# Cross-attention and expert mixture on one core: four gathers of 512 KB begun by two queues, queries made earlier, x loaded ahead of the gathers

## The reference

```
qk  = einsum('bhdq,bhdl->bhql', qh, kh) / sqrt(128)
ret = einsum('bhql,bhdl->bhdq', softmax(qk), vh)
x   = x + gamma * ret
```

```
h     = relu(xn @ W1 + b1);  alpha = softmax(h @ W2 + b2)
out   = sum_k alpha_k * U_k (V_k xn);   x = x + out
```

## Time and profile before

| | |
|---|---|
| median of 3 runs | 1813.11 us (1811.18 to 1814.56) |
| profiled execution | 1809.29 us, its span 1807.5 us |
| busy PE / VectorE / ScalarE / GpSimd | 1610.1 / 986.1 / 772.3 / 717.3 us |
| granted TensorE clock, mean | 0.967 |
| DMA moved by the sync queue | 293.87 MB |
| gather DMAs | 1024 of 128 KB, 2.8 us to landing |

### The profile page before, as it was taken

One profiled execution on the slowest core, in us unless ns is written; L12 is line 12 of the kernel. 1 busy time (PEld: TensorE's weight loads), 2 busy tenths in 40 slices (PEclk: granted clock), 3 DMA queues, 4 the chain that ended last, 5 costly groups with the idle time before them and its releaser, 6 DMA issues.

```text
span 1807.5 us, 22223 instructions
## 1 busy us (share of the span) xinstructions
PE 1610.1 (89%) x6496; PEld 1181.8 (65%) x6496; DVE 986.1 (55%) x1290; ACT 772.3 (43%) x1222; POOL 717.3 (40%) x523
## 2 busy tenths in 40 slices
PE   5888888887878888888887599999999999999999
PEld 3555555565656565656554478777787878787877
DVE  6767676768676777777776353242333333233312
ACT  5656565656656565656565341212212121212120
POOL 3767776777767777767675200000000000000000
PEclk9999999999999999999999799999999999999999
DMA  5877878778877878888877612112120303121202
GB/s 177 232 240 239 243 239 239 231 243 244 246 237 237 246 239 242 245 247 239 251 221 232 234 69 93 47 62 79 37 102 6 133 0 104 35 93 46 93 1 70
DMA packets 128155, 294.22 MB, mean 163 GB/s; under 512 B 34432, under 2 KB 39552, under 8 KB 128128
## 3 DMA queue, kind: packets, MB, share of 16 engines
q1 hardware_dynamic: 128128, 293.87, 53.2%
HBM read 125.87 MB, written 33.69 MB: 88 GB/s over the span
## 4 chain that ended last, share of the span: by engine, by line
PE 48%; SPq 16%; DVE 12%; DMA 9%; issue 8%; POOL 4%; ACT 1%; DVEq 0%; ACTq 0%; POOLq 0%
PE scores L929 19%; SPq L223 14%; PE scores L972 10%; PE attended L990 10%; DMA x_raw<-in_x 8%; DVE neg_max L571 6%; DVE pb L580 4%; POOL pt_lo L342 3%; PE scores L517 2%; PE spare L1009 2%; PE attended L539 1%; PE attended L542 1%; PE scores L944 1%; PE scores L947 1%; SPq L234 1%
## 5 line engine op out<-in xcount | busy, mean ns | idle before, releaser
L342 POOL TENSOR_TENSOR pt_lo<-pt,pt_hi 128x512 fp32r<-128x512 f32 (+1 forms) x256 | 399.9, 1563 | 247.2 <-ACT pt_hi L411 246.3
L418 ACT ACTIVATE probs<-scores,neg_max 128x1024 f32<-128x1024 f32 x256 | 285.8, 1117 | 322.6 <-DVE neg_max L571 322.5
L571 DVE TENSOR_REDUCE neg_max<-scores 128x1 f32<-128x1024 f32 x256 | 310.9, 1214 | 64.5 <-PE scores L517 63.8
L517 PE MATMUL scores<-k_hi,q_hi 128*128 128x512 f32 x512 | 235.8, 542 | 121.0 <-ACT probs L418 111.8
L580 DVE STREAM_TRANSPOSE pb<-probs 128x1024 f32<-128x1024 f32 x256 | 315.5, 1232 | 0.1
L854 POOL TENSOR_TENSOR rstd<-var_eps,minus_half 128x1 f32<-128x1 f32 x28 | 17.2, 615 | 609.4 <-DVE var_eps L1055 609.4
L517 PEld LDWEIGHTS scores<-k_hi,q_hi 128*128 128x128 f32 x512 | 97.7, 198 | 234.7 <-ACT probs L418 142.4
L411 ACT ACTIVATE pt_hi<-pt 128x512 fp32r<-128x512 f32 (+1 forms) x256 | 186.5, 728 | 56.4 <-DMA pt<-pb 56.4
L539 PE MATMUL attended<-pt_hi,v_hi 128*128 128x512 f32 x320 | 144.8, 453 | 70.0 <-POOL pt_lo L342 69.3
L542 PE MATMUL attended<-pt,v_nat 128*128 128x512 f32 x384 | 205.4, 617 | 0.0
L929 PE MATMUL scores<-nt_hi,w_hi 128*128 128x512 f32 x512 | 200.9, 392 | 2.5 <-DVE w_lo L1080 2.5
(11 more groups left out here) (95 smaller groups left out, 2709.2 us busy)
## 6 DMA issues: line engine op xcount, KB each, us to landing
pt<-pb SPq DMA_DIRECT2D x1024, 128.0 KB, 2.8
x_raw<-in_x SPq DMA_DIRECT2D x32, 512.0 KB, 5.6
k_raw<-in_ctx SPq DMA_DIRECT2D x32, 512.0 KB, 4.5
gain_row<-gains SPq DMA_DIRECT2D x64, 256.0 KB, 4.7
x_res<-in_x SPq DMA_DIRECT2D x32, 512.0 KB, 4.7
x<-x_out SPq DMA_DIRECT2D x64, 256.0 KB, 3.8
first_n<-x SPq DMA_DIRECT2D x32, 512.0 KB, 3.7
result<-x SPq DMA_DIRECT2D x64, 256.0 KB, 3.9
```

Source lines behind the costliest of these rows:

```text
L342: nc.gpsimd.tensor_tensor(pt_lo[2 * parity + half][:, :, keys, :], pt[2 * parity + half][:, :, keys, :], as_f32(hi[half][q][:]), ALU.subtr ...
L418: nc.scalar.activation(probs[j % 2][:], scores[j % 2][:], ACT.Exp, bias=neg_max[:, j:j + 1], accum_out=row_sum[b][:, j:j + 1]).then_inc(s_ ...
L517: last = mm(scores[j % 2][:, c * BANK:(c + 1) * BANK], q[b][:, queries], k[b][:, c * BANK:(c + 1) * BANK], start=(i == 0), stop=(i == 2))
L571: nc.vector.tensor_reduce(neg_max[:, j:j + 1], scores[j % 2][:], AX_X, ALU.max, negate=True).then_inc(s_max, 1)
```

## The change

The gather of a half becomes four DMAs of 512 KB, one for each source quadrant. The sync queue begins quadrants 0 and 1 where it began all 16 before. ScalarE begins quadrants 2 and 3: those of the last head's half 1 in block 1, after its `pt_hi`, and those of this head's half 0 in block 5. The semaphore's count for a gather goes from 256 to 64. On the sync queue the load of x for head h + 2 is moved ahead of the gather of half 0. ScalarE's `queries` and `high_queries` move from block 5 to block 3; VectorE's `variance` from block 3 to block 2, ahead of the scaling of attended; `scale_of_queries` from block 4 to 2 and `low_queries` from block 6 to 5 on GpSimd.

```diff
-    GATHERS = QB * QB * 16
+    GATHERS = QB * 16
@@ sync queue, gather
-            for g in range(QB):
-                for a in (0, 2, 1, 3):
-                    sp.dma_start(dst[g:P:QB, a, :, :].rearrange("p k n -> p (k n)"),
-                                 pb[half][SB * a:SB * a + SB, JB * g:JB * g + JB, :, :].rearrange(
-                                     "p k j c -> p (k j c)")).then_inc(s_gather[half], 16)
+            for a in range(QB // 2):
+                sp.dma_start(dst[:, a, :, :].rearrange("p k n -> p (k n)"),
+                             pb[half][SB * a:SB * a + SB, :, :, :].rearrange("p (g k) j c -> p g (k j c)", g=QB)
+                             ).then_inc(s_gather[half], 16)
@@ sync queue, slot
+            if more:
+                sp.wait_ge(s_q32, h + 2)
+                load_x(h + 2)
             gather(h, n, 0, parity)
             if not first:
                 spread_gain(h - 1, 1)
-            if more:
-                sp.wait_ge(s_q32, h + 2)
-                load_x(h + 2)
@@ GpSimd, slot
-                if j == 4 and not last:
+                if j == 2 and not last:
                     scale_of_queries(h + 1, 1 - parity)
-                if j == 6 and not last:
+                if j == 5 and not last:
                     low_queries(h + 1, 1 - parity)
@@ ScalarE
+        def gather(h, n, half, parity):
+
+            act.wait_ge(s_blocks, n + 4 * half + 4)
+            dst = pt[2 * parity + half]
+            for a in range(QB // 2, QB):
+                act.dma_start(dst[:, a, :, :].rearrange("p k n -> p (k n)"),
+                              pb[half][SB * a:SB * a + SB, :, :, :].rearrange("p (g k) j c -> p g (k j c)", g=QB)
+                              ).then_inc(s_gather[half], 16)
@@ ScalarE, slot
-                if j == 5 and not last:
+                if j == 1 and not first:
+                    gather(h - 1, n - JB, 1, 1 - parity)
+                if j == 5:
+                    gather(h, n, 0, parity)
+                if j == 3 and not last:
                     queries(h + 1, 1 - parity)
                     high_queries(h + 1, n + JB, 1 - parity)
@@ ScalarE, after the slots
+        gather(h - 1, n - JB, 1, 1)
         gains(h - 1, 0)
@@ VectorE, slot
-                if j == 3 and not last:
+                if j == 2 and not last:
                     dve.wait_ge(s_stat, h * 2 + 4)
...
+                if j == 2 and not last:
+                    variance(h + 1, 1 - parity)
                 if j == 2 and not early:
                     scale_attended(h - 2, n - 2 * JB, 1)
-                if j == 3:
-                    if not last:
-                        variance(h + 1, 1 - parity)
-                    if not first:
-                        inverse_sums(h - 1, 1, 1 - parity)
+                if j == 3 and not first:
+                    inverse_sums(h - 1, 1, 1 - parity)
```

## The result

The changed kernel takes 1826.72 us (median of 4 runs, 1823.01 to 1828.85) against 1812.14 before: a ratio of 1.0077 with a 95% interval of 1.0056 to 1.0098. It is slower by 0.8%, where 1634 us and a range of 1598 to 1690 were forecast. The profiled execution has a span of 1827.0 us. PE's granted clock over the run is 0.959, before it was 0.967.

What follows compares the result with a forecast made beforehand. No engine was taken as full: a loop through the sync queue's issue time and one late x load was the bound. 30 periods x 5.3 = 159 us plus 20 at the edges gave 179 us less: 1634 us, range 1598 to 1690.

Steps and rivals of the forecast that it cites:

- What bounds the kernel now: Attention stage: no engine full, but a loop through the sync queue's issue time and one late x load; period 30.51 us.
- The x load: Sync queue: x issued ahead of the gather, ending VectorE's stall of 6.2 us a head, 191.2 us in all.
- cover of 4.2 us: Time left for other traffic between x landing at 517.8 and VectorE first asking for it at 521.99.
- The gather on the sync queue: 16 issues become two of 0.6 us, so the queue is held 1.2 us instead of 10.2, twice a head.
- The gather on ScalarE: Blocks 1 and 5: four issues a head of 0.6 us, mostly fitting where ScalarE waited for the maxima.
- Rivals B and C: B: ScalarE's issues about 1.5 us each, 1712 us, chance 0.08; C: ScalarE held at every issue, 1880 us, chance 0.04.
- What is late next: PE's 23.4 us plus waits give 25.2 us a head; its block 5 pt_lo wait grows from 0.84 to about 1.5.
- Do the gathers land in time?: Next block 0: about 8.8 us available, 3 MB take 7.9 us at 397 GB/s; about 1.3 us lateness absorbed.
- Rival A: Gathers late: both halves together at 205 GB/s, so splitting quarter 0 ends the loop; 84 us more, 1718 us, chance 0.14.
- The port rule: Partitions 0 to 63 reach half of 16 DMA ports: sync queue's pair about 218 GB/s, full rate needing ScalarE's beside it.
- Edges: First and last slots: x wait 5 us less, VectorE's first_n wait 8 less, PE's last pt_lo wait 7 less.

Runs made afterwards that it cites:

- x ahead alone: Kernel after without its gather part: x load ahead and the reordering kept, 16 gathers of 128 KB a half on the sync queue; 1734.06 us, ratio 0.956.
- plain copies: Kernel after with every gather replaced by a same-size copy from each partition to the same partition (wrong values); 1647.36 us, ratio 0.9088.
- mixed pairs: Kernel after, but the sync queue takes quadrants 0 and 2 and ScalarE 1 and 3; 1792.24 and 1808.85 us.

## Why the prediction was wrong, point by point

- **What bounds the kernel now**: right. x ahead alone gives 0.956.
- **The x load**: the wait of 191.2 us was to vanish; after it is 72.5, or 2.5 us in each of 29. The cover of 4.2 us was eaten from two sides. The sync queue's store and residual issues, held for 2.46 and 2.11 us, let x go out at 524.32, 5.5 us before VectorE was ready for it (531.84 - 2.00), where 10.4 were forecast; and it took 7.5 us to land, not 6.2. With plain copies x lands in a median of 7.2 us and the wait is gone, so the late issue weighs more than the landing.
- **The gather on the sync queue**: "size hardly counts, and the sync queue is held 1.2 us". Wrong in the kernel after: single gather issues took a median of 1.0 and up to 4.7 us, the x load's a median of 2.6, and a gain's up to 4.0. Right with plain copies, 1.26 and 1.12 us for two.
- **The gather on ScalarE**: 0.6 us an issue was right (median 0.62 of 128, longest 3.6), and so was that it costs nothing: 25.61 us a head with plain copies. Rivals B and C are out.
- **What is late next**: 25.2 us a head against 25.61 measured where the DMA engines are not the limit, and PE's wait in block 5 1.19 us for the 1.5 forecast.
- **Do the gathers land in time?** This is the step that failed: "at the 397 GB/s reached where a gather ran beside a load that is 7.9 us ... I take the fast end." The 397 were one microsecond of a gather and the residual load together, and the row doesn't say how much was the gather. The row of the gather alone said 201 GB/s at a DMA share of 0.72; I read "not full". Divided, it is 201 / 0.72 = 280 GB/s for the old form (two queues made 270 of it alone, at a share of 0.87), and nothing at all was known of the new one. Measured alone, the new form makes 236 GB/s as the kernel begins it, and 167 to 236 over all orders. The transfer time of a whole head was never summed: with these rates it is 26.2 us, with the slowest full order 30.8, in both cases above PE's 23.4 and the forecast's 25.2. In place of 25.2 the runs show 31.27 us with the gathers and 25.61 with plain copies of the same size, so the missed term, what the gather's transfers cost beyond plain copies, is 5.7 us a head. The sum by the kernel's own form gives 0.6 of it (26.2 less 25.61); where the other 5.1 come from is open.
- **Rival A** named the mechanism with too small a price, and its sign came: ScalarE's wait for the gather of 5.90 us at 504.41. It took 205 GB/s for the two halves and let only one wait grow; in the kernel residual, x, `pb` and pt are late together. Its own row, 2 MB in 10.2 us, twice a head and 3.0 MB besides at 357 GB/s, adds up to 29 us. I never made that sum, though it would have been too high for the old form: the kernel with x ahead only moves the same bytes in 27.95 us a head.
- **The port rule** stood in the text, and was allowed to count only if ScalarE's pair did not overlap the other. The pairs overlapped in part: in half 1 the sync queue's went out from 500.26, and each landed 8.0 to 8.2 us after its issue, ScalarE's from 504.87; in half 0 ScalarE's from 518.16, landing after 6.5 and 9.9 us, the sync queue's from 526.79. That "the full rate needs ScalarE's pair beside it" must not be read as if the pair would bring it: two queues on opposite halves made 236 GB/s with 512 KB gathers, 254 with copies and 270 with 128 KB gathers, and nothing here shows 376 for them.
- **Edges**: the wait for first_n fell from 8.27 to 4.24 us, the last pt_lo wait from 14.97 to 12.06, where 8 and 7 less were forecast. These 7 us in all are too small to be taken apart. The granted clock, forecast at 1.0 throughout, was 0.94 from 200 to 800 us; with plain copies it was 1.00.

Still open: why the kernels with two queues of 512 KB gathers take 4 to 5 us a head more than their bytes and rates give; why both halves, read at once by two queues, give 254 and not 376 GB/s; why a single gather takes 3.2 us longer than a plain copy, where the half rate gives 1.5; and why the kernel with mixed pairs on two queues has two rhythms.

## What to carry to other kernels

Before an issue-bound stream of DMAs is made quicker to issue, ask what the DMA engines could move in that form: measure the new form alone, and sum bytes over rate for the whole loop, loads included, as for any engine. Take the sum as a first check and not as the answer: for the 512 KB gathers it was right to 4% with one queue and 4 to 5 us short of 31 with two. A DMA share of 0.8 in the old loop is no spare fifth if the new form costs more time a byte. Small transfers in an order that changes between the halves of the partitions can beat one large transfer of the same bytes (1680 us against 1827 here), and the order of two numbers in a loop can be worth 5%.

## What the runs showed of the hardware

- SBUF to SBUF copies of 64 partitions: 0 to 63 at 181 GB/s, 32 to 95 at 346; 0 to 63 beside 64 to 127 from a second queue, 254 together.
- One quadrant at a time read to HBM 227 GB/s, written from HBM 199; all partitions 380 and 357. The reversed gather (128 partitions to one quadrant) 116.
- With the DMA engines 0.95 busy, a DMA's issue on the sync queue took up to 5.6 us in place of 0.35 to 0.6 (x load, median 2.6; a gain of 2 KB up to 4.0).
- Two queues move more of the 128 KB gathers than one: 270 GB/s against 196. The Trainium skill (DMA: Bandwidth & Descriptors, Issuing engines are not separate DMA queues) says that beginning DMAs on several engines only saves sequencer time, which is usually small. Here that time was the limit of one queue: 0.64 us for 128 KB, 205 GB/s.
